# Quantised layer of a decoder: gate and up products from fp32r halves, and fewer VectorE passes around them

## The reference

```python
def act_qdq(x):
    qmax = 2.0 ** (ACT_BITS - 1) - 1.0
    scale = jnp.maximum(jnp.max(jnp.abs(x)) / qmax, 1e-12)
    return jnp.clip(jnp.round(x / scale), -qmax - 1.0, qmax) * scale

def fixed_qdq_u16(x):
    scale = 1.0 / 65536.0
    return jnp.clip(jnp.round(x / scale), 0.0, 65535.0) * scale
```

## Time and profile before

| | |
|---|---|
| median of 3 runs | 6057.34 us (6056.36 to 6064.21) |
| profiled execution, its own time | 6057.39 us |
| its span | 6055.7 us |
| busy: PE, DVE, ACT, POOL | 76%, 64%, 47%, 33% |
| mean granted TensorE clock | 0.873 of full speed |
| this layer in the span | about 955 to 1532 us |

### The profile page before, as it was taken

One profiled execution on the slowest core, in us unless ns is written; L12 is line 12 of the kernel. 1 busy time (PEld: TensorE's weight loads), 2 busy tenths in 40 slices (PEclk: granted clock), 3 DMA queues, 4 the chain that ended last, 5 costly groups with the idle time before them and its releaser, 6 DMA issues. The chain is left out here.

```text
span 6055.7 us, 94426 instructions
## 1 busy us (share of the span) xinstructions
PE 4584.0 (76%) x24898; PEld 2861.8 (47%) x24898; DVE 3893.7 (64%) x8139; ACT 2858.2 (47%) x6148; POOL 2021.5 (33%) x3169
## 2 busy tenths in 40 slices
PE   6577773928789748996757677887676977995897
PEld 3244432417433327872336455776455853334434
DVE  5566666386388764443779766569766556885566
ACT  1366662143257633234545456335465324773353
POOL 0244430000176412223435542225541215542342
PEclk8798996969889879997779889999898998997897
DMA  5788871000533202104522321012321035323533
GB/s 176 252 304 307 306 250 53 0 0 0 184 100 93 76 12 78 43 25 127 154 78 106 119 81 37 22 40 106 117 81 35 7 109 149 88 72 102 171 117 103
DMA packets 326728, 648.04 MB, mean 107 GB/s; under 512 B 72914, under 2 KB 140148, under 8 KB 326345
## 3 DMA queue, kind: packets, MB, share of 16 engines
q1 hardware_dynamic: 259256, 463.30, 23.2%
q0 software_dynamic: 67104, 180.70, 10.3%
HBM read 361.41 MB, written 251.28 MB: 101 GB/s over the span
## 5 line engine op out<-in xcount | busy, mean ns | idle before, releaser
L813 DVE TENSOR_REDUCE t_nmax<-t_aps 128x2 f32<-128x1024 f32 x700 | 837.7, 1222 | 278.0 <-PE t_aps L735 272.6
L920 ACT ACTIVATE t_expT<-t_bps 128x512 f32<-128x512 f32 x1290 | 701.5, 599 | 283.2 <-PE t_bps L754 234.5
L754 PE MATMUL t_bps<-t_Q,t_K 51*128 51x512 f32 (+2 forms) x1290 | 524.7, 468 | 61.3 <-ACT t_expT L920 43.0
L735 PE MATMUL t_aps<-t_K,t_Q 49*128 49x512 f32 (+2 forms) x1400 | 463.1, 459 | 63.8 <-DMA t_K<-k_halves 28.7
L754 PEld LDWEIGHTS t_bps<-t_Q,t_K 51*128 51x128 f32 (+2 forms) x1290 | 228.0, 189 | 528.6 <-ACT t_expT L920 372.1
L2097 DVE TENSOR_TENSOR f_hl<-f_h,f_hh 128x512 fp32r<-128x512 f32 x192 | 203.7, 1061 | 411.4 <-ACT f_hh L2022 411.4
L781 PE MATMUL t_ops<-t_expT,t_V 128*17 128x512 f32 (+1 forms) x2560 | 413.8, 614 | 0.4 <-ACT t_expT L920 0.4
L3514 ACT ACTIVATE t_relsb<-t_relsb,t_nmax 128x128 f32<-128x128 f32 (+3 forms) x512 | 288.7, 564 | 220.0 <-DVE t_nmax L3486 219.5
L2386 POOL TENSOR_TENSOR a_crossed<-a_qsb,a_tab 128x256 f32<-128x256 f32 x272 | 266.3, 1000 | 294.0 <-ACT a_qsb L2333 263.0
L3392 POOL TENSOR_TENSOR t_relsb<-t_relsb,t_M 128x128 f32<-128x128 f32 x512 | 216.6, 454 | 387.7 <-DMA t_relsb<-rel 387.7
L854 POOL DMA_DIRECT2D t_Q<-q_halves x525 | 270.9, 518 | 147.3 <-POOLq L78 73.8
(11 more groups left out here) (439 smaller groups left out, 12455.8 us busy)
## 6 DMA issues: line engine op xcount, KB each, us to landing
rel<-t_rows SPq DMA_DIRECT2D x128, 640.0 KB, 4.4
t_relsb<-rel SPq DMA_DIRECT2D x128, 640.0 KB, 6.3
t_Q<-q_halves POOLq DMA_DIRECT2D x420, 64.0 KB, 2.5
t_K<-k_halves POOLq DMA_DIRECT2D x420, 64.0 KB, 2.6
k_halves<-a_parts SPq DMA_DIRECT2D x48, 512.0 KB, 4.8
q_halves<-a_parts SPq DMA_DIRECT2D x48, 512.0 KB, 5.6
o_xT<-attended SPq DMA_DIRECT2D x32, 512.0 KB
f_R<-combine SPq DMA_DIRECT2D x128, 128.0 KB, 2.9
```

What stands on the lines that cost most here:

```text
L735: last = nc.tensor.matmul(aps[:, (t * PPG + i) % 2, x, :], operand(Qr, KA, p, h, slice(t * P, (t + 1) * P)), operand(Kr, KA, p, h, slice(0 ...
L754: nc.tensor.matmul(bps[:, slot_of(kb, j), :], operand(Kr, KB, p, h, slice(kb * P, (kb + 1) * P)), operand(Qr, KB, p, h, slice(0, S)), star ...
L813: nc.vector.tensor_reduce(nmax[:, g, t, i * HPT:(i + 1) * HPT], aps[:, (t * PPG + i) % 2], AX.X, ALU.max, negate=True).then_inc(s["maxed"], 1)
L920: nc.scalar.activation(expT[:, kb % RING, j, :], bps[:, slot_of(kb, j), :], ACT.Exp).then_inc(s["expo"], 1 + (PAD if end else 0))
```

## The change

The gate and up weights and the turned `x` are split in two parts each, a high one (`gh`, `uh`, `xh`: the value rounded to fp32r) and the rest (`gl`, `ul`, `xl`). A product is then six matmuls on fp32r operands over the two 128-feature halves (`triple`): high with high, low weight with high `x`, high weight with low `x`; low with low is left out. ACT makes `xh` (`upper`), POOL makes `xl` by a subtraction (`lower`), in `f1a` and again in `f1c`. `dequantise` makes three or four transposes into one bank, four banks in turn, and splits the weights there. In `f1b` the clip is done in the same DVE operation as the rounding. In `f1c` the scale of `up` goes into the scale of `hidden` (`both`), so that one DVE pass is left out and the constant is subtracted inside the product; `up` is one buffer of a whole batch, and ACT rounds it in tiles of 512.

```diff
-def dequantise(nc, G, name, wg, wu, wd, gT, uT, dT):
-
-    with phase(nc, name, "w ready turned copied dvc") as (s, sb, ps):
+def dequantise(nc, G, name, wg, wu, wd, gh, gl, uh, ul, dT, room):
+    with phase(nc, name, "w ready turned copied lower dvc") as (s, sb, ps):
         NBK = 48
-        raw = sb("raw", [P, 3, NBK, 32])
+        raw = room[:, 0:3 * NBK * 32].rearrange("p (w n k) -> p w n k", n=NBK, k=32)
         amax = sb("amax", [P, 3, NBK])
         sc = sb("sc", [P, 3, NBK])
         inv = sb("inv", [P, 3, NBK])
-        wps = ps("wps", [P, 2, S])
+        wps = ps("wps", [P, 4, S])
...
+            def turns():
+                for i, hi, lo in ((0, gh, gl), (1, uh, ul)):
+                    v = raw[:, i].rearrange("p (o n) k -> p o (n k)", n=8)
+                    for k in range(2):
+                        for o in (0, 3):
+                            cols = slice(o * P, (o + 3) * P)
+                            yield [v[:, o + m, k * P:(k + 1) * P] for m in range(3)], hi[:, k, cols], lo[:, k, cols]
+                v = raw[:, 2].rearrange("p (o n) k -> p o (n k)", n=24)
+                for k in (0, 2, 4):
+                    yield [v[:, o, m * P:(m + 1) * P] for m in (k, k + 1) for o in range(2)], dT[:, k:k + 2, :].rearrange("p k d -> p (k d)"), None
...
+                for n, (srcs, hi, lo) in enumerate(turns()):
+                    if lo is not None:
+                        dve.wait_ge(s["copied"], n + 1)
+                        nc.vector.tensor_tensor(lo.bitcast(F32R), wps[:, n % 4, 0:len(srcs) * P], hi, ALU.subtract).then_inc(s["lower"], 1)
             @block.tensor
             def _(pe):
                 pe.wait_ge(s["ready"], 1)
...
+                for n, (srcs, hi, lo) in enumerate(turns()):
+                    if n >= 4:
+                        pe.wait_ge(s["lower" if n - 4 < 8 else "copied"], n - 3)
+                    for m, src in enumerate(srcs):
+                        last = nc.tensor.transpose(wps[:, n % 4, m * P:(m + 1) * P], src, G.ident[:, :])
+                    last.then_inc(s["turned"], 1)
             @block.scalar
             def _(act):
-                for n, (src, dst) in enumerate(turns()):
+                for n, (srcs, hi, lo) in enumerate(turns()):
                     act.wait_ge(s["turned"], n + 1)
-                    nc.scalar.copy(dst, wps[:, n % 2, 0:P]).then_inc(s["copied"], 1)
-
+                    nc.scalar.copy(hi if lo is None else hi.bitcast(F32R), wps[:, n % 4, 0:len(srcs) * P]).then_inc(s["copied"], 1)
...
+        uparts = sb("upT", [P, 2, KT, FT * P])
...
+        gates = ctx.enter_context(ExitStack())
+        gparts = gates.enter_context(nc.sbuf_tensor("gateT", [P, 2, KT, FT * P], F32))
+        gh, gl, uh, ul = gparts[:, 0], gparts[:, 1], uparts[:, 0], uparts[:, 1]
...
+        def fast(x):
+            return x.bitcast(F32R)
+        def triple(pe, s, o, wh, wl, xh, xl, b, m):
+            cols = slice(m * P, (m + 1) * P)
+            for i, (w, k) in enumerate(((wh, 0), (wl, 0), (wh, 1), (wl, 1))):
+                nc.tensor.matmul(o, fast(w[:, k, cols]), fast(xh[:, b % 2, k]), start=i == 0, stop=False)
+            for k in range(KT):
+                if m == 0:
+                    pe.wait_ge(s["lo"], b * KT + k + 1)
+                last = nc.tensor.matmul(o, fast(wh[:, k, cols]), fast(xl[:, (b * KT + k) % 3]), start=False, stop=k == KT - 1)
+            return last
+        def lower(pool, s, xh, xl, b):
+            pool.wait_ge(s["hi"], b + 1)
+            for k in range(KT):
+                c = b * KT + k
+                if c >= 3:
+                    pool.wait_ge(s["u"], ((c - 3) // KT + 1) * FT)
+                nc.gpsimd.tensor_tensor(fast(xl[:, c % 3]), xT[:, k, b * S:(b + 1) * S], xh[:, b % 2, k], ALU.subtract).then_inc(s["lo"], 1)
+        with phase(nc, "f1a", "hi lo g u g_cp g_mx u_mx") as (s, psb, ps):
+            xh = psb("xh", [P, 2, KT, S])
+            xl = psb("xl", [P, 3, S])
             gps = ps("gps", [P, 4, S])
             ups = ps("ups", [P, 4, S])
             with nc.Block() as block:
                 @block.tensor
                 def _(pe):
-                    with pe.Fori(0, NB) as b:
+                    for b in range(NB):
+                        pe.wait_ge(s["hi"], b + 1)
                         for m in range(FT):
                             n = b * FT + m
...
+                            if n >= 4:
+                                pe.wait_ge(s["g_cp"], n - 3)
+                            triple(pe, s, gps[:, n % 4, :], gh, gl, xh, xl, b, m).then_inc(s["g"], 1)
+                            if n >= 4:
+                                pe.wait_ge(s["u_mx"], n - 3)
+                            triple(pe, s, ups[:, n % 4, :], uh, ul, xh, xl, b, m).then_inc(s["u"], 1)
                 @block.scalar
                 def _(act):
-                    act.sem_inc(s["g_cp"], 2)
-                    with act.Fori(0, NB) as b:
+                    def upper(b):
+                        if b >= 2:
+                            act.wait_ge(s["u"], (b - 1) * FT)
+                        nc.scalar.copy(fast(xh[:, b % 2]), xT[:, :, b * S:(b + 1) * S]).then_inc(s["hi"], 1)
+                    upper(0)
+                    upper(1)
+                    for b in range(NB):
                         for m in range(FT):
-                            act.wait_ge(s["g"], b * FT + m + 1)
-                            nc.scalar.copy(act_[:, m, ds(b * S, S)], gps[:, m % 2, :]).then_inc(s["g_cp"], 1)
+                            n = b * FT + m
+                            act.wait_ge(s["g"], n + 1)
+                            nc.scalar.copy(act_[:, m, b * S:(b + 1) * S], gps[:, n % 4, :]).then_inc(s["g_cp"], 1)
+                            if m == 1 and 1 <= b < NB - 1:
+                                upper(b + 1)
+                @block.gpsimd
+                def _(pool):
+                    for b in range(NB):
+                        lower(pool, s, xh, xl, b)
                 @block.vector
                 def _(dve):
-                    dve.sem_inc(s["u_mx"], 2)
-                    with dve.Fori(0, NB) as b:
+                    for b in range(NB):
                         for m in range(FT):
...
+                            n = b * FT + m
+                            dve.wait_ge(s["u"], n + 1)
+                            nc.vector.tensor_reduce(mx[:, 1, n:n + 1], ups[:, n % 4, :], AX.X, ALU.max, apply_absolute_value=True).then_inc(s["u_mx"], 1)
+                        dve.wait_ge(s["g_cp"], (b + 1) * FT)
+                        nc.vector.tensor_reduce(mx[:, 2, b:b + 1], act_[:, :, b * S:(b + 1) * S], AX.XY, ALU.max, apply_absolute_value=True).then_inc(s["g_mx"], 1)
+        gates.close()
         grid(nc, G, "f1h", [mx[:, 1, :], mx[:, 2, 0:NB]], [1, 2])
...
                     def weigh(i):
-                        base = i * 8
+                        base = i * 6
                         for x in range(2):
                             dve.wait_ge(s["sig"], i * 2 + x + 1)
-                            nc.vector.tensor_scalar(sg[:, x], sg[:, x], 65536.0, MAGIC, ALU.mult, ALU.add).then_inc(s["weighed"], 1)
+                            nc.vector.tensor_scalar(sg[:, x], sg[:, x], 65535.0 / 65536.0, MAGIC / 65536.0, ALU.min, ALU.add).then_inc(s["weighed"], 1)
                         for x in range(2):
                             dve.wait_ge(s["weighed"], base + 1 + x)
-                            nc.vector.tensor_scalar(sg[:, x], sg[:, x], MAGIC, 65535.0, ALU.subtract, ALU.min).then_inc(s["weighed"], 1)
+                            nc.vector.scalar_tensor_tensor(half(i, x), sg[:, x], MAGIC / 65536.0, half(i, x), ALU.subtract, ALU.mult).then_inc(s["weighed"], 1)
                         for x in range(2):
                             dve.wait_ge(s["weighed"], base + 3 + x)
-                            nc.vector.scalar_tensor_tensor(half(i, x), sg[:, x], 1.0 / 65536.0, half(i, x), ALU.mult, ALU.mult).then_inc(s["weighed"], 1)
-                        for x in range(2):
-                            dve.wait_ge(s["weighed"], base + 5 + x)
                             nc.vector.tensor_reduce(mx[:, 3, ds(i * 2 + x, 1)], half(i, x), AX.XY, ALU.max, apply_absolute_value=True).then_inc(s["weighed"], 1)
...
-                                act.wait_ge(s["weighed"], before * 8 + 5 + x)
+                                act.wait_ge(s["weighed"], before * 6 + 3 + x)
...
-        with phase(nc, "f1c", "u u_cp pre set whole product") as (s, psb, ps):
-            up = psb("up", [P, 2, FT, W2])
+        with phase(nc, "f1c", "hi lo u u_cp pre set whole product peak") as (s, psb, ps):
+            up = psb("up", [P, FT, S])
+            xh = psb("xh", [P, 2, KT, S])
+            xl = psb("xl", [P, 3, S])
             magic = psb("magic", [P, 1])
+            both = psb("both", [P, 1])
             ups = ps("ups", [P, 4, S])
+            def piece(b, x):
+                return act_[:, :, b * S + x * W2:b * S + (x + 1) * W2]
```

(76 more changed lines are left out.)

52 lines of the change are left out of this document (1 added, 51 removed).

## The result

| | executions | median us | lowest to highest |
|---|---|---|---|
| before | 16 | 6065.76 | 6050.85 to 6089.41 |
| after | 16 | 6037.00 | 6021.51 to 6060.94 |

The ratio is 0.9948 (95% interval 0.9934 to 0.9961): 31.5 us less, between 24 and 40; the two medians themselves are 28.8 apart. The forecast was 34.2 less, but it was taken from 6057.4, and so it gave 6023 where 6037 was measured, 3 us above the end of its range. The interval holds the change that was forecast. The level that it started from was off.

What follows compares the result with a forecast made beforehand. The layer was read phase by phase, f1a bound by PE's matmuls, f1b by DVE's passes, f1c by PE with DVE and ACT close: -7.4 - 16.2 - 13.9 + 3.3 = -34.2, from 6057.4 to 6023 us, range 6007 to 6034.

Steps and rivals of the forecast that it cites:

- `f1w`'s transposes to the last copy: In f1w, 36 transposes no longer each wait for a copy: minus 7.4 us, bounds 5 and 8.2.
- f1g's mark to f1h's: Between the first two all-reduce starts, f1a's cheaper matmuls less POOL's delays: minus 16.2 us.
- f1h's to f1i's: Between the second and third all-reduce starts, f1b loses one DVE pass, 1.74 us, 8 times: minus 13.9 us.
- f1i's to f1j's: Between the third and fourth all-reduce starts, f1c with POOL's subtractions and one up buffer: 100.4 us for 97.1, plus 3.3.
- the stall: In f1a, PE waits each batch for a free xl slot: 0.5 us, seven times, 3.5 in all.
- The 4 us and nine matmuls at the lower clock: At f1a's start after PE's pause, 9 matmuls take 0.43 us and not 0.23: plus 1.9 us.
- 216 ns: Rival: one-pass matmuls take 216 ns, so 576 give 7.6 us less and f1c nothing: 6015.6 us, chance 0.04.
- the batch of 9.6: In f1c, a batch's chain through ACT and DVE, with a scaling meeting POOL's subtraction: 9.6 us, ends 8.6 and 10.5.
- the head: Start of f1c, from the all-reduce through POOL's code change (7.4) to the first pair of products: 24.3 us.
- New rows on POOL for free: Rival: POOL's code is loaded once and kept, so its new rows cost nothing: 6000 us, chance 0.10.
- Nothing gained and POOL dearer: Rival: POOL's change costs 8.3 us at all four places and f1c's batches take 10.5: 6034 us, chance 0.08.
- The clock in `f1c`: Rival: PE's pauses in every f1c batch hold it at the lower clock: 6069 us, slower, chance 0.03; sign: clock below 0.9.

Runs made afterwards that it cites:

- the layer alone: Kernels before and after, each with only its quantised layer (stage 1), the other layers left out: 615.31 us and 582.08, 33.2 less.
- warm_pool: Kernel after plus three small POOL instructions with unread results (product in f1t, all-reduce at the end of f1a and f1c): ratio 0.9925 to the kernel before.

## Why the forecast missed, and where it was right

**The step that failed** is the base: "The sum is made against the profiled execution's own time, 6057.39 us, which is the median of the runs (6057.34) within 0.1 us." Three executions that agree within 8 us looked like a level. They were three of the sixteen in the result's own comparison, whose median is 6065.76: 8.4 higher. From there the same sum gives 6031.6, inside the range. That is 8.4 of the 13.8 us by which 6023.2 missed 6037.0. The other 5.4 are the change itself, 28.8 by the medians where 34.2 was forecast; the interval (24 to 40) holds both, the layer alone gave 33.2, and whether there is more in it than chance stays open. Of 79 executions of this program in all the comparisons, the median is 6069.5, the ends 6041.8 and 6093.9, the standard deviation 11.0, and only 12 were as low as 6057.4. The range fails for the same reason: it adds up the bounds of the layer's terms and has none for the level, though a scatter of 11 us is wider than any of them. That a measurement "tells 0.2% (12 us) from no change" stood in the text, and wasn't used for the range.

**The terms**, against the profiles of both kernels:

| step | forecast | measured |
|---|---|---|
| `f1w`'s transposes to the last copy | -7.4 | 15.12 to 6.96: -8.2 |
| f1g's mark to f1h's | -16.2 | 190.3 to 174.5: -15.8 |
| f1h's to f1i's | -13.9 | 104.8 to 90.9: -13.9 |
| f1i's to f1j's | +3.3 | 97.1 to 101.6: +4.6 |
| sum | -34.2 | -33.3; the layer alone -33.2 |

That the sum agrees to 1 us is in part luck: `f1w`'s -0.8 takes back some of `f1c`'s +1.3, and the first span before varies by 3 us from profile to profile. (`f1w`'s transposes before filled a quarter of their slot, 128 of 512 columns, not half.)

`f1a`: POOL's pause behind `f1t` was 7.8 (7.4 taken), the stall 0.54 a batch (0.5), the matmul 16.37 / 72 = 0.227 without a stall (0.229), `f1h`'s all-reduce 6.6 behind the end of DVE's last maximum in `f1a` (6.49). The 4 us and nine matmuls at the lower clock, 1.9 us, rest on no row that was shown. The kernel after has 16 such matmuls: the seventeenth starts 13.4 us after PE's first, with a wait of 5.3 in between. By the GPSIMD Engine Reference of the Trainium skill (Instruction dispatch) the first call of freshly loaded code pays 5.95 us; the three all-reduces with nothing else to wait for, 5.56, 5.83 and 6.17, agree, while the way back is longer, 7.2 (8.27 less the 1.07 after which ACT starts). The 216 ns that the Trainium skill gives for a matmul by itself (TensorE: Matmul & The Clock Gate, Back-to-back issue gap) aren't reached here in 576 of them: 227.

`f1c`: the batch of 9.6 came out at 9.61, and for the reason given, a scaling that meets POOL's subtraction and takes 2.10 for 1.01. By the SBUF page of the Trainium skill (SBUF — State Buffer, Who interferes with whom), of two instructions that need the shared ports the one that issues first has them for its whole length, and the other waits. That fits: POOL's subtraction at 1337.71 stands just ahead of the scaling, which takes 1.09 more, and the next one, at 1339.17, meets the scaling's end and takes 1.79; POOL's mean was 1.46 here and 1.28 in `f1a`. That POOL's own time hardly moves, which the prediction took from another layer, didn't hold. The missing 1.3 us is in the head: the first pair of products ended 25.7 after the all-reduce and not 24.3. POOL began 0.4 later than taken, PE needed 0.5 more for the six tiles, and the pair took 3.81 and not 3.4, with one of POOL's subtractions (1321.04) beside it.

**The rivals.** New rows on POOL for free: out, by the marks and by `warm_pool`. 216 ns: out. Nothing gained and POOL dearer: out as it was put, since the batches took 9.6 and not 10.5, and the all-reduces came 5.6 behind DVE; what is true of it is that `f1c` lost. The clock in `f1c`: the mean of 0.87 is below the 0.9 that I had named as a sign of it, but it comes from the head alone, as two windows of the phase show (the clock is the third number from the end):

```profile
1300.00:1317.00 17.00, 8.72 (x20) 6.07 (x21) 2.52 (x6) 9.92 (x9) 4.06 (x4) 0.52 0.00 0
1317.00:1388.00 71.00, 65.00 (x270) 49.20 (x268) 66.19 (x42) 56.38 (x64) 19.55 (x13) 1.00 0.00 1
```

In every batch two matmuls start 1.18 us apart (1339.84 and 1341.02) where 0.23 is usual; that didn't lower the clock.
